# Two graph layers on one core: the small constants in ScalarE's queue, and block 1 of rows 0 multiplied by x2 in the first pass

## The chip, the cores and the metric

The kernel runs on one core of a Trainium2 chip. The time is device microseconds of one execution; the median of several executions is what two versions are compared by. All arithmetic is float32.

## What is computed

There are 4096 nodes with 128 features each, and `adj` is a dense 4096 x 4096 matrix. Two layers follow each other, each with a residual and a layer norm:

```python
# layer 1: graph convolution, layer norm, then a Mamba block over the 4096 rows
h = relu(adj @ x @ gcn_w + gcn_b)
h = (h - mean(h)) * rsqrt(var(h) + 1e-5) * ln_g + ln_b
xz = h @ w_in                              # 128 -> 512: xc and z
u  = silu(causal_conv4(xc) + conv_b)
dt = softplus((u @ w_xp)[:, :8] @ w_dt + b_dt);  B, C = the next 16 + 16 columns
hst = exp(dt * A) * hst + dt * B * u       # a scan over the rows, 256 x 16 states
y  = (hst @ C + u * D_skip) * silu(z)
x1 = layernorm(x + y @ w_out)
# layer 2: the same adj against x1 and against x2, a 3-layer MLP each, then a merge
out1 = mlp(W1, b1, (2 + eps1) * (adj @ x1));  out2 = mlp(W2, b2, (2 + eps2) * (adj @ x2))
out  = layernorm(x1 + concat(out1, out2) @ Wm.T + bm)
```

So `adj` has to be multiplied by three 4096 x 128 operands: x, x2 and x1. The first two are known from the start. Of x1, 512 rows become known each time that a chunk of the scan is done.

## The kernel before

**Tiling.** `adj` (transposed) is cut in 8 x 8 blocks of 512 x 512, 1 MB each. A block in `LOADS` is written (parts, n, m): n is the stripe of 512 result rows, m the stripe of 512 operand rows, and the parts are the operands it is multiplied by: `X` = x, `X2` = x2, `X1` = x1, `ONE` = x and x2 from one load, `DOUBLE` = x2 and x1 from one load. One part of a block is 4 matmuls of 128x128 against 128x512 (`JT` = 4). The profile writes each such float32 matmul as two (x2). A block of one part is 4 matmuls per megabyte loaded, a block of two parts is 8.

**Ring.** SyncE (SP) loads the blocks in the order of `LOADS` into four places of `ring`; load i waits until block i-4 has been used (`s_blk_used`). Blocks 0 and 1 come in four pieces each.

**The ramp.** Rows 0 of `adj @ x` (blocks 0 to 7) are computed first, since the whole chain of chunk 0 depends on them. `BOTH` = 1 says that of these only block 0 is multiplied by x2 too. VectorE (DVE) copies that partial sum of x2 out of its PSUM bank into `kept`, and it is added when the other x2 parts of rows 0, for m = 1 to 7, are done in chunk 3. Behind the ramp stand the steps gcn, in_x, x_proj and dt of chunk 0, filled up with 32 matmuls of `FILL_BLOCKS`.

**Chunks.** Chunk c is 512 rows of the scan: 16 units, one for each state, of which each takes exponentials of ScalarE (ACT, `p_dA`), two scans and a product of DVE, and two multiplications or additions of GpSimd (POOL). TensorE (PE) works on the matrix blocks at the same time: `CHUNK_BLOCKS[c]` names the blocks of each chunk, `spread_blocks` cuts their matmuls into 32 halves of units so that each half has about the same share of matmuls and steps, and `chain_steps` says in which half each of the other PE steps stands. For chunk c these are `z` of c, `out` of c-1 (c-1's y by w_out), then `gcn`, `in_x`, `x_proj` and `dt` of c+1, and the four steps of an x2 MLP, `mlp0` to `mlp3`. Each engine runs its own program in its written order. Between the PE steps of chunk c+1 the work goes through the other engines: from `gcn` to `in_x` through DVE (`stats`, lines 1102 to 1112), ACT (`norm`, 782 to 794), DVE (`turn`, 1117) and ACT (`moves`, 803, into `hr`); from `dt` to the next scans through ACT (850 to 858) and DVE (1141, 1148).

**The end of a chunk.** DVE ends unit 15 with the addition behind `mlp3` (line 1171, into `resid`) and begins unit 0 of the next chunk with two scans (line 1035). ACT follows each scan with the next exponential (line 737), and then, where a sum of x1 parts in `p_two` was closed in the unit before (`SUMS`), copies it out (line 974, `acc`). The second matmul of step `z` (line 605) writes `p_two` and so waits for this copy (`sum_taken(last_two(n, 0))`).

**Constants.** Six small loads, `w_dt` twice (9 x 256), `scale1`, `scale2` (128 x 1), `bm`, `gb` (128 x 128), stand in SP's queue between the loads of block 7 and block 8. ACT's queue holds the loads of x (and x2 for block 0) and the first part of `pack`; behind these ACT loads a table and waits for `pack`.

Of the kernel before, what the change touches and what calls it, by code (L numbers as in the profile page):

```python
# [13 lines left out]
JT = T // P  # L14
# [3 lines left out]
R = 8  # L18
# [8 lines left out]
KEEP = 5  # L27
EPS = 1e-5
PIECES = 2
BOTH = 1  # L30
END_ACT = range(2)
STAGES = 4
MOVES_0 = 2
# [6 lines left out]
ROW_DT = (0, 64)  # L40
# [19 lines left out]
def row(what, n, columns):  # L60
    return [(what, n, m) for m in columns]
# [3 lines left out]
ONE, X, X2, X1, DOUBLE = ("x", "x2"), ("x",), ("x2",), ("x1",), ("x2", "x1")  # L65


def mixed(*lists):
# [12 lines left out]
    row(ONE, 3, ALL[2:]) + row(ONE, 4, ALL[:4]),  # L81
    row(ONE, 4, ALL[4:]) + row(X, 5, ALL) + row(X1, 2, (0, 1)) + row(X, 6, (0,)) + row(X1, 3, (0, 1)),
    row(X, 6, (1,)) + row(X1, 4, (0, 1)) + mixed(row(X, 6, ALL[2:]), row(X2, 0, (3, 4, 5)))
    + row(X2, 0, (6, 7, 1, 2)) + row(X1, 0, (0, 1, 2)) + row(X, 7, (0,)),
    row(X, 7, (1,)) + row(DOUBLE, 1, (0, 1)) + mixed(row(X, 7, ALL[2:]), row(X2, 1, ALL[4:])) + row(DOUBLE, 1, (2, 3))
    + row(X1, 5, (0,)),
    row(X2, 5, (0,)) + row(DOUBLE, 5, ALL[1:4]) + row(X1, 5, (4,)) + row(X2, 5, (4, 5)) + row(X1, 2, (2, 3, 4)) + row(X2, 5, (6, 7))
# [184 lines left out]
def two_layer_graph_kernel(nc, blocks, x_d, x2_d, pack_d, w_dt_d, eps1_d, eps2_d, bm_d, gb_d, rows_d, out_d):  # L272
    ctx = ExitStack()
    with ctx:
# [38 lines left out]
        w_dt = sb("w_dt", [P, G * P])  # L313
# [153 lines left out]
        @block.sync  # L467
        def _(sp_):
            def load(i):
                _, n, m = LOADS[i]  # L470
                wait(sp_, s_blk_used, i - RING + 1)
                sp_.dma_start(ring[:, i % RING, :, :], blocks[n, m]).then_inc(s_blk[i % RING], 16)

            def load_x2(k):
                sp_.dma_start(x2_s[:, JT * k:JT * (k + 1), :], x2_d[k]).then_inc(s_x2s[k], 16)


            for i in range(PIECES):
                for jt in range(JT):
                    sp_.dma_start(ring[:, i, jt, :], blocks[0, i, :, jt]).then_inc(s_tile[JT * i + jt], 16)  # L480
            for k in range(PIECES, NBLK):
                load(k)
            for row in ROW_DT:
                sp_.dma_start(w_dt[row:row + R + 1, :], w_dt_d).then_inc(s_wdt, 16)
            sp_.dma_start(scale1[:, :], eps1_d).then_inc(s_consts_in, 16)
            sp_.dma_start(scale2[:, :], eps2_d).then_inc(s_consts_in, 16)
            sp_.dma_start(bm[:, :], bm_d).then_inc(s_consts_in, 16)
            sp_.dma_start(gb[:, :], gb_d).then_inc(s_consts_in, 16)
            for k in range(NBLK):
                load(NBLK + k)  # L490
                if k - 2 >= BOTH:
                    load_x2(k - 2)
            sp_.dma_start(pack[:, PACK_LATE:PACK_W], pack_d[:, PACK_LATE:PACK_W]).then_inc(s_late, 16)
            for k in range(NBLK - 2, NBLK):
                load_x2(k)
            for i in range(2 * NBLK, len(LOADS)):
                load(i)
            for k in range(NC - 2):
                sp_.wait_ge(s_fin, k + 1)
                sp_.dma_start(out_d[k], stage(k)).then_inc(s_out[k % STAGES], 16)  # L500
            k = NC - 1
            for h in range(2):
                tiles = slice(h * JT // 2, (h + 1) * JT // 2)
                sp_.wait_ge(s_fin_dve, h + 1)
                sp_.dma_start(out_d[k][:, tiles, :], stage(k)[:, tiles, :]).then_inc(s_out[k % STAGES], 16)
            for q in range(STAGES):
                sp_.wait_ge(s_out[q], 16 * (NC // STAGES + (q == k % STAGES)))

        @block.tensor
        def _(pe):  # L510
# [49 lines left out]
            def block_part(i, lo, hi, chunk=NC - 1, unit=S):  # L560
                steps = block_steps(LOADS[i])
                if lo == 0 and i >= PIECES:
                    pe.wait_ge(*filled(i))
                for q in range(lo, hi):
                    part, jt = steps[q]
                    last = second(i, jt, chunk, unit) if part == "x1" else first(i, part, jt)
                    if q == len(steps) - 1:
                        last.then_inc(s_blk_used, 1)
                    elif part in ("x", "x2") and jt == JT - 1 and i == LAST_OF[part, LOADS[i][1]]:
                        last.then_inc(s_px if part == "x" else s_px2, 1)  # L570
# [92 lines left out]
            for k in range(1, NBLK):  # L663
                pe.wait_ge(s_xs[k], 16)
                if k < PIECES:
                    for jt in range(JT):
                        pe.wait_ge(s_tile[JT * k + jt], 16)
                        block_part(k, jt, jt + 1)
                else:
                    block_part(k, 0, JT)  # L670
            pe.wait_ge(s_pack, 16)
# [58 lines left out]
        def _(act):  # L730
# [193 lines left out]
            for k in range(1, NBLK):  # L924

                if k == 2:
                    act.wait_ge(s_tile[1], 32)
                elif k in (3, 4):
                    act.wait_ge(s_tile[3 * k - 7], 16)
                elif k > 4:  # L930
                    act.wait_ge(*filled(k - 3))
                act.dma_start(x_s[:, JT * k:JT * (k + 1), :], x_d[k]).then_inc(s_xs[k], 16)
            act.dma_start(pack[:, 0:PACK_LATE], pack_d[:, 0:PACK_LATE]).then_inc(s_pack, 16)
            act.preload_act_table_set(LOG_EXP)
            act.wait_ge(s_pack, 16)
            act.activation(A[:, :, :], w("A_log").rearrange("p (g s) -> p g s", g=G), ACT.Exp).then_inc(s_A, 1)
# [449 lines left out]
```

## Time and profile before

| what | value |
|---|---|
| median of 3 runs | 802.83 us (802.69 to 803.57) |
| the profiled execution: time / span | 801.87 / 800.1 us |
| granted clock of TensorE | 0.999 of full |
| PE, DVE, ACT, POOL busy | 791.8, 626.9, 437.9, 620.3 us |
| PE share of the chain that ended last | 93% |
| DMA moved | 231.6 MB, mean 289 GB/s |

The span lies inside the time: 1.77 us of the profiled execution are around it. Rows begin with the start in us and the duration; a bracket at the end says how long the engine had been idle before the instruction and what ended that. PEld is TensorE's weight load, which runs beside the matmuls. An idle time that ends in "issue" is one in which nothing that the profile shows was waited for.

### The profile page before, as it was taken

The numbers are of one execution on the slowest core, as the hardware profiler recorded it, in microseconds if no ns is written. First come the engines' busy times: TensorE is split into PE (matmuls) and PEld (weight loads), VectorE is DVE, ScalarE is ACT, GpSimd is POOL, SyncE is SP. The second block draws the span as 40 slices with busy tenths as digits, with TensorE's granted clock in tenths as the row PEclk, the third lists the DMA queues.
The fourth block names the chain that finished last, engine by engine and source line by source line (L and its number), as shares of the span: only waits on it lengthen the run. The fifth ranks groups of instructions, "written<-read, shape, count | busy, mean of one in ns | idle before, by whom it ended". The sixth has DMA issues, their size and how long they took to land.

```text
span 800.1 us, 7650 instructions
## 1 busy us (share of the span) xinstructions
PE 791.8 (99%) x2100; PEld 364.4 (46%) x2100; DVE 626.9 (78%) x882; ACT 437.9 (55%) x827; POOL 620.3 (78%) x300
## 2 busy tenths in 40 slices
PE   9999999999999999999999999999999999999996
PEld 4444444444454444544454445444544454444454
DVE  0045989999998988989999998988989888982135
ACT  0165576477647764676467645863475646331235
POOL 0004999999998989899989997979789899980036
PEclk9999999999999999999999999999999999999999
DMA  8999767775766999999979977899778896887602
GB/s 334 373 342 366 234 251 252 255 255 214 266 217 193 359 378 359 339 368 375 369 255 366 374 265 246 318 349 381 262 262 290 299 349 215 303 314 273 252 26 80
DMA packets 64254, 231.61 MB, mean 289 GB/s; under 512 B 7490, under 2 KB 8532, under 8 KB 45396
## 3 DMA queue, kind: packets, MB, share of 16 engines
q1 hardware_dynamic: 25236, 160.72, 53.2%
q10 hardware_dynamic: 38976, 70.41, 26.9%
q8 instruction: 17, 0.28, 0.1%
q14 instruction: 25, 0.20, 0.1%
HBM read 228.48 MB, written 2.62 MB: 289 GB/s over the span
## 4 chain that ended last, share of the span: by engine, by line
PE 93%; DMA 2%; ACT 2%; DVE 2%; ACTq 0%; issue 0%; DVEq 0%
PE p_x L527 51%; PE p_x L557 16%; PE p_two L557 11%; PE p_m L628 2%; PE p_m L644 2%; PE p_dA L727 2%; DMA spread_C<-bc_rows 2%; PE p_two L618 1%; PE p_m L611 1%; PE p_m L593 1%; PE p_m L648 1%; PE p_m L640 1%; PE p_two L598 1%; DMA x_s<-x_tiles 1%; PE p_m L586 1%; PE p_h L727 1%
## 5 line engine op out<-in xcount | busy, mean ns | idle before, releaser
L527 PE MATMUL p_x<-ring,x_s 128*128 128x512 f32 x1024 | 453.8, 594 | 0.2 <-DMA x_s<-x_tiles 0.2
L1281 POOL TENSOR_TENSOR bh<-spread,dtu 128x1024 f32<-128x1024 f32 x127 | 300.4, 2366 | 37.9 <-DVE bh L1224 36.1
L1290 POOL TENSOR_TENSOR y<-y,prod 128x1024 f32<-128x1024 f32 x120 | 283.2, 2360 | 47.9 <-DVE prod L1048 39.4
L527 PEld LDWEIGHTS p_x<-ring,x_s 128*128 128x128 f32 x1024 | 192.1, 190 | 243.6 <-issue 240.1
L1035 DVE TENSOR_TENSOR_SCAN p_h<-p_dA,state,bh 128x512 f32<-128x512 f32 x224 | 276.1, 1278 | 21.5 <-ACT p_dA L737 8.6
L737 ACT ACTIVATE p_dA<-dt,A 128x512 f32<-128x512 f32 x256 | 172.0, 686 | 133.2 <-DVE p_h L1035 132.5
L1048 DVE TENSOR_TENSOR prod<-p_h,spread_C 128x1024 f32<-128x1024 f32 x120 | 145.7, 1214 | 5.6 <-DMA spread_C<-bc_rows 4.6
L557 PE MATMUL p_x<-ring,x 128*128 128x512 f32 x304 | 136.9, 592 | 0.0
L557 PE MATMUL p_two<-ring,x 128*128 128x512 f32 x208 | 94.2, 593 | 0.0
L557 PEld LDWEIGHTS p_x<-ring,x 128*128 128x128 f32 x304 | 57.4, 190 | 71.6 <-issue 71.6
L432 POOL TENSOR_SCALAR dtu<-prod,mv,rstd 128x128 f32<-128x128 f32 x26 | 20.4, 802 | 59.2 <-ACT rstd L1001 59.2
L557 PEld LDWEIGHTS p_two<-ring,x 128*128 128x128 f32 x208 | 38.9, 190 | 47.5 <-issue 47.5
L1083 DVE TENSOR_TENSOR acc<-p_x,acc 128x512 f32<-128x512 f32 x17 | 11.7, 687 | 41.2 <-PE p_x L557 41.2
L1035 DVE TENSOR_TENSOR_SCAN p_h<-p_dA,bh 128x512 f32<-128x512 f32 x32 | 37.5, 1218 | 2.6 <-ACT p_dA L737 1.5
L803 ACT ACTIVATE hr<-turned 32x128 f32<-32x128 f32 x120 | 36.9, 307 | 3.2 <-DVE turned L1117 0.8
L887 ACT ACTIVATE mb<-p_m,pack 128x512 f32<-128x512 f32 x16 | 11.0, 687 | 26.2 <-PE p_m L644 25.8
L1319 POOL COPY wx<-pack 128x16 f32<-128x16 f32 x1 | 0.2, 198 | 31.0 <-DMA pack<-pack_w 31.0
L1045 DVE COPY state<-p_h 128x2 f32<-128x2 f32 x112 | 16.8, 150 | 6.6 <-DVE p_h L1035 0.5
L1073 DVE SCALAR_TENSOR_TENSOR p_m<-xcv,pack,p_m 128x512 f32<-128x512 f32 x24 | 18.0, 749 | 4.1 <-ACT p_m L820 3.6
L1207 DVE TENSOR_SCALAR pack<-pack 128x512 f32<-128x512 f32 x1 | 0.5, 486 | 24.2 <-PE p_h L674 24.2
L1073 DVE SCALAR_TENSOR_TENSOR p_two<-xcv,pack,p_two 128x512 f32<-128x512 f32 x24 | 18.1, 753 | 0.6
L1141 DVE SCALAR_TENSOR_TENSOR p_two<-p_two,dt 128x512 f32<-128x512 f32 x8 | 5.6, 700 | 15.7 <-ACT dt L854 15.7
(141 smaller groups left out, 611.1 us busy)
## 6 DMA issues: line engine op xcount, KB each, us to landing
ring<-adj_blocks SPq DMA_DIRECT2D x147, 1024.0 KB, 7.2
spread_C<-bc_rows ACTq DMA_DIRECT2D x128, 256.0 KB, 6.4
spread<-bc_rows ACTq DMA_DIRECT2D x127, 256.0 KB, 5.2
ring<-adj_blocks SPq DMA_DIRECT2D x8, 256.0 KB, 6.7
x_s<-x_tiles ACTq DMA_DIRECT2D x7, 256.0 KB, 8.9
x_s<-x_tiles SPq DMA_DIRECT2D x7, 256.0 KB, 7.6
out_tiles<-dtu SPq DMA_DIRECT2D x6, 256.0 KB, 2.0
pack<-pack_w SPq DMA_DIRECT2D x1, 640.0 KB, 8.0
```

The lines of the kernel that those rows point to most:

```text
L432: last = eng.tensor_scalar(stage(k)[:, q, :], last_r(k)[:, q, :], mv[:, k % 4, q, 0:1], rstd[:, k % 4, q:q + 1], ALU.subtract, ALU.mult)
L527: return pe.matmul(bank[:, :], tiles[:, JT * m + jt, :], ring[:, i % RING, jt, :], start=opens, stop=closes)
L557: return pe.matmul(sum_bank(no)[:, :], x1[:, m % KEEP, jt, :], ring[:, i % RING, jt, :], start=opens, stop=closes)
L727: pe.matmul(bank, W1[:, l, :], moving[:, columns], start=True, stop=True).then_inc(s_l, 1)
L737: act.activation(p_dA[g][:, :], dt_[:, c % 2, g, :], ACT.Exp, scale=A[:, g, unit:unit + 1]).then_inc(s_dA, 1)
L803: last = act.activation(hr4[Q * r:Q * (r + 1), :, Q * q:Q * (q + 1)], turned[Q * q:Q * (q + 1), :, Q * r:Q * (r + 1)], ACT.Copy)
L1035: dve.tensor_tensor_scan(p_h[:, g, :], p_dA[g][:, :], bh[:, i % 3, g, :], first, ALU.mult, ALU.add).then_inc(s_scan, 1)
L1045: dve.tensor_copy(state[:, unit, :], p_h[:, :, T - 1]).then_inc(s_state, 1)
L1048: dve.tensor_tensor(prod[:, i % 2, :, :], p_h[:, :, :], both(spread_C[:, i % SLOTS_C, :]), ALU.mult).then_inc(s_cmul, 1)
L1073: dve.scalar_tensor_tensor(out=bank[:, :], in0=xcv[:, g, k:k + T], scalar=conv_w[:, g, k:k + 1], in1=bank[:, :], op0=ALU.mult, op1=ALU.add ...
L1281: pool.tensor_tensor(bh[:, i % 3, :, :], both(spread[:, q, :]), dtu[:, c % 2, :, :], ALU.mult).then_inc(s_bmul, 1)
L1290: pool.tensor_tensor(y[:, c % 2, :, :], y[:, c % 2, :, :], prod[:, i % 2, :, :], ALU.add).then_inc(s_acc, 1)
```

## The change

Three things are changed. `BOTH` becomes 2: block 1 is now (x, x2) too. PE takes its four pieces by turns, first by x, then by x2, and DVE copies the sum out after block 1. The x2 rows for it (256 KB) are loaded in ACT's queue right behind the x rows of block 1; in SP's queue the load of these same x2 rows, after block 11, is gone. In chunk 3 the single-part block (x2, 0, 1) is dropped, and block (x, 7, 0) moves ahead of the three x1 blocks. The number of matmuls is the same; there is one block load of 1 MB less (148 instead of 149). Third, the six small constants move from SP's queue to ACT's, behind `pack`, `gb` first.

```diff
-BOTH = 1
+BOTH = 2
...
-    + row(X2, 0, (6, 7, 1, 2)) + row(X1, 0, (0, 1, 2)) + row(X, 7, (0,)),
+    + row(X2, 0, (6, 7, 2)) + row(X, 7, (0,)) + row(X1, 0, (0, 1, 2)),
...
                 load(k)
-            for row in ROW_DT:
-                sp_.dma_start(w_dt[row:row + R + 1, :], w_dt_d).then_inc(s_wdt, 16)
-            sp_.dma_start(scale1[:, :], eps1_d).then_inc(s_consts_in, 16)
-            sp_.dma_start(scale2[:, :], eps2_d).then_inc(s_consts_in, 16)
-            sp_.dma_start(bm[:, :], bm_d).then_inc(s_consts_in, 16)
-            sp_.dma_start(gb[:, :], gb_d).then_inc(s_consts_in, 16)
...
                         block_part(k, jt, jt + 1)
+                        if k < BOTH:
+                            if jt == 0:
+                                pe.wait_ge(s_x2s[k], 16)
+                            block_part(k, JT + jt, JT + jt + 1)
...
                 act.dma_start(x_s[:, JT * k:JT * (k + 1), :], x_d[k]).then_inc(s_xs[k], 16)
+                if k < BOTH:
+                    act.dma_start(x2_s[:, JT * k:JT * (k + 1), :], x2_d[k]).then_inc(s_x2s[k], 16)
             act.dma_start(pack[:, 0:PACK_LATE], pack_d[:, 0:PACK_LATE]).then_inc(s_pack, 16)
+
+            act.dma_start(gb[:, :], gb_d).then_inc(s_consts_in, 16)
+            for row in ROW_DT:
+                act.dma_start(w_dt[row:row + R + 1, :], w_dt_d).then_inc(s_wdt, 16)
+            act.dma_start(scale1[:, :], eps1_d).then_inc(s_consts_in, 16)
+            act.dma_start(scale2[:, :], eps2_d).then_inc(s_consts_in, 16)
+            act.dma_start(bm[:, :], bm_d).then_inc(s_consts_in, 16)
```

How PE's program moves is shown by its instruction order (lines up to 660 of the kernel before are 6 higher than in the changed one). An `x17` is 17 matmuls; x2_s and its bank p_x2 are written as x_s and p_x. First the ramp, on PE, from the start, before:

```order
L655 MATMUL p_m<-sq 128x256 x4
L527 MATMUL p_x<-ring,x_s 128x512 x36
L674 MATMUL p_h<-pack 128x1 x4
L586 MATMUL p_m<-pack,ax 128x128 x4
L527 MATMUL p_x<-ring,x_s 128x512 x11
```

and now:

```order
L649 MATMUL p_m<-sq 128x256 x4
L521 MATMUL p_x<-ring,x_s 128x512 x40
L672 MATMUL p_h<-pack 128x1 x4
L580 MATMUL p_m<-pack,ax 128x128 x4
L521 MATMUL p_x<-ring,x_s 128x512 x11
```

Four matmuls more stand ahead of the first chunk's chain; what stands behind them is the same. Second, PE in chunk 3, from `gcn` (L586) through `in_x` (L593, L598), `x_proj` (L611) and `dt` (L618) to `mlp0` (L640), before:

```order
L586 MATMUL p_m<-pack,ax 128x128 x4
L527 MATMUL p_x<-ring,x_s 128x512 x17
L593 MATMUL p_m<-hr,pack 128x512
L598 MATMUL p_two<-hr,pack 128x512
L527 MATMUL p_x<-ring,x_s 128x512 x15
L611 MATMUL p_m<-u,wx 64x512 x2
L527 MATMUL p_x<-ring,x_s 128x512 x8
L618 MATMUL p_two<-dbc,w_dt 128x512
L618 MATMUL p_m<-dbc,w_dt 128x512
L527 MATMUL p_x<-ring,x_s 128x512 x11
L640 MATMUL p_m<-ax,pack 128x512
```

and now (the same steps under L580, L587, L592, L605, L612, L634):

```order
L580 MATMUL p_m<-pack,ax 128x128 x4
L521 MATMUL p_x<-ring,x_s 128x512 x15
L587 MATMUL p_m<-hr,pack 128x512
L592 MATMUL p_two<-hr,pack 128x512
L521 MATMUL p_x<-ring,x_s 128x512 x15
L605 MATMUL p_m<-u,wx 64x512 x2
L521 MATMUL p_x<-ring,x_s 128x512 x7
L612 MATMUL p_two<-dbc,w_dt 128x512
L612 MATMUL p_m<-dbc,w_dt 128x512
L521 MATMUL p_x<-ring,x_s 128x512 x11
L634 MATMUL p_m<-ax,pack 128x512
```

Two matmuls are gone between `gcn` and `in_x`, one between `x_proj` and `dt`. Third, PE at the end of chunk 3, from `mlp2` (L644) through `mlp3` (L648) to `z` of chunk 4 (L603, L605), before:

```order
L644 MATMUL p_m<-mb,pack 128x512
L557 MATMUL p_two<-ring,x 128x512 x3
L527 MATMUL p_x<-ring,x_s 128x512 x2
L648 MATMUL p_m<-pack,mb 128x128 x4
L527 MATMUL p_x<-ring,x_s 128x512 x5
L603 MATMUL p_m<-hr,pack 128x512
L605 MATMUL p_two<-hr,pack 128x512
```

and now:

```order
L638 MATMUL p_m<-mb,pack 128x512
L551 MATMUL p_two<-ring,x 128x512 x4
L642 MATMUL p_m<-pack,mb 128x128 x4
L551 MATMUL p_two<-ring,x 128x512 x2
L521 MATMUL p_x<-ring,x_s 128x512 x3
L597 MATMUL p_m<-hr,pack 128x512
L599 MATMUL p_two<-hr,pack 128x512
```

One matmul is gone ahead of `mlp3`; between `mlp3` and `z` there are five as before, but the x1 sum in `p_two` is closed two matmuls behind `mlp3`. From `z` to `gcn` of this chunk there are 10 matmuls as before (three now, four before, ahead of `out`).

## Rows read from the trace of the kernel before

**Rows 1.** The page, part 1: busy time, share, instructions.

```profile
PE 791.8 (99%) x2100; PEld 364.4 (46%) x2100; DVE 626.9 (78%) x882; ACT 437.9 (55%) x827; POOL 620.3 (78%) x300
```

**Rows 2.** Timeline of PEld in the ramp.

```profile
15.62 0.19 PEld L527 LDWEIGHTS p_x<-ring,x_s 128*128 128x128 f32 x1 [0.24 <-issue]
16.20 0.47 PEld L527 LDWEIGHTS p_x<-ring,x_s 128*128 128x128 f32 x2 [0.39 <-issue]
```

**Rows 3.** Waits of PEld, whole span: waited for, us in total, times, longest.

```profile
PEld p_x L527 <- issue: 240.1, 969, 0.8
...
PEld p_x L527 <- DMA x_s<-x_tiles: 3.0, 4, 1.0
PEld p_m L593 <- ACT hr L803: 1.6, 2, 1.0
```

**Rows 4.** Timeline of PE in chunk 3.

```profile
328.94 14.76 PE L527 MATMUL p_x<-ring,x_s 128*128 128x512 f32 x34
343.54 1.02 PE L593 MATMUL p_m<-hr,pack 128*128 128x512 f32 x2
...
397.53 1.02 PE L605 MATMUL p_two<-hr,pack 128*128 128x512 f32 x2
398.39 3.60 PE L527 MATMUL p_x<-ring,x_s 128*128 128x512 f32 x8
```

**Rows 5.** Timeline of PE, the ramp and the first chain.

```profile
8.65 28.59 PE L527 MATMUL p_x<-ring,x_s 128*128 128x512 f32 x66 [0.18 <-DMA x_s<-x_tiles]
...
48.74 1.13 PE L593 MATMUL p_m<-hr,pack 128*128 128x512 f32 x2
49.70 1.02 PE L598 MATMUL p_two<-hr,pack 128*128 128x512 f32 x2
```

**Rows 6.** Busy time by engine in the ramp; last: granted clock, DMA share, GB/s.

```profile
10.00:15.00 5.00, 5.00 (x13) 2.28 (x12) 0.69 (x1) 0.00 (x0) 0.00 (x0) 1.00 1.01 404
```

**Rows 7.** Timeline of the queues of SP and ACT, and ACT, 22 to 33 us.

```profile
23.91 0.72 SPq L484 DMA_DIRECT2D w_dt<-w_dt_rows  x2
...
26.02 0.43 SPq L488 DMA_DIRECT2D gb<-gcn_b_in  x1
...
26.98 10.63 SPq L472 DMA_DIRECT2D ring<-adj_blocks  x4
...
32.92 0.23 ACT L936 ACTIVATE A<-pack 128x32 f32<-128x32 f32 x1 [8.34 <-DMA pack<-pack_w]
```

**Rows 8.** Busy time by engine in chunk 3, first `z` to next `z`.

```profile
315.70:396.67 80.97, 80.96 (x215) 36.88 (x214) 74.42 (x99) 51.82 (x99) 75.38 (x33) 1.00 0.97 362
```

**Rows 9.** Timeline of DVE in chunk 3, where it waited for PE.

```profile
323.10 0.69 DVE L1152 TENSOR_TENSOR dbc<-p_m,x_s 128x512 f32<-128x512 f32 x1 [0.51 <-PE p_m L628]
...
329.14 0.70 DVE L1102 SCALAR_TENSOR_TENSOR p_m<-gb,p_m 128x512 f32<-128x512 f32 x1 [0.30 <-PE p_m L586]
...
370.75 0.70 DVE L1141 SCALAR_TENSOR_TENSOR p_two<-p_two,dt 128x512 f32<-128x512 f32 x1 [0.99 <-ACT dt L854]
...
392.58 0.69 DVE L1171 TENSOR_TENSOR resid<-p_m,bm 128x512 f32<-128x512 f32 x1 [0.75 <-PE p_m L648]
393.19 2.46 DVE L1035 TENSOR_TENSOR_SCAN p_h<-p_dA,state,bh 128x512 f32<-128x512 f32 x2
```

**Rows 10.** Timeline of ACT in chunk 3.

```profile
341.55 0.31 ACT L803 ACTIVATE hr<-turned 32x128 f32<-32x128 f32 x1
...
366.21 0.45 ACTq L756 DMA_DIRECT2D spread_C<-bc_rows  x1
367.45 0.60 ACT L850 ACTIVATE dt<-p_two 128x512 f32<-128x512 f32 x1 [0.92 <-PE p_m L618]
...
396.66 0.60 ACT L974 ACTIVATE acc<-p_two 128x512 f32<-128x512 f32 x1 [0.29 <-issue]
```

**Rows 11.** Timeline of POOL, last addition of chunk 3.

```profile
387.52 2.37 POOL L1290 TENSOR_TENSOR y<-y,prod 128x1024 f32<-128x1024 f32 x1
```

## Prediction, made before the run

> **What bounds the kernel now.** I read the busy line first, then the waits of the weight load, then stretches of the timeline. PE is busy 99% of the span [rows 1]. A busy PE need not be a full one, so I look at the weight loads: one every 0.43 us, 0.19 busy and 0.24 idle that ends in "issue" [rows 2], 969 times on this line [rows 3]. 34 passes (17 matmuls) take 14.6 us from their start to the start of the next row [rows 4], again 0.43 each. So a matmul costs two passes, 0.858 us, and PE gives one after the other without a gap in nearly all of the span. The true waits are few: 3.0 us on the operands of the first block, 1.6 us in two waits for `hr` [rows 3]. As long as the other engines deliver in time, the time is PE's work plus these, and moving four matmuls from one place to another changes nothing. The question is whether the others deliver in time in the stretch that becomes shorter.
>
> The Trainium skill, "Perfetto Trace Analysis", section "Identifying Performance Opportunities", says that headroom on the tensor engine is to be judged by the busy share of the weight loads, and on Vector and GpSimd by occupancy. By the first PE would be half empty (46%), and the four matmuls might go in free; this trace disagrees, since a pass comes each 0.43 us for 28.59 us on end [rows 5].
>
> **The ramp: +3.43 us, -0.15 us.** Four matmuls more stand ahead of `gcn` of chunk 0: 4 x 0.858 = 3.43 us. The whole first chain stands behind them, and it has the same 32 filler matmuls, so nothing hides them there; they are owed back by chunk 3. What the ramp may win: PE waits for the operands of block 0 until 8.65 [rows 5]. These are ahead of the new x2 load in ACT's queue, so this stays. The weight load at 16.20 comes 0.15 later than the cadence (0.39 instead of 0.24 idle, [rows 2]), where block 2 begins; block 1 now takes 6.86 us instead of 3.43, and block 2 has landed by then: -0.15. The 256 KB more at 3 us, at the 404 GB/s that the full DMA engines move there [rows 6], may push block 1's last pieces and block 2 back by 0.65 us. Block 1's last piece is now needed 2.6 us later than before and block 2 3.4 us later, so this is hidden; without that cover it would cost up to 0.65. The wait of PE for `hr` at 48.74 (the next row starts 0.96 behind it instead of 0.86, [rows 5]) is set by the chain from `gcn` on and moves with it.
>
> **The six constants: 0.** SP issues them from 23.91 until 26.45 and issues block 8 at 26.98 [rows 7]. The four ring loads from there on take their places from PE, one each 3.43 us; block 8 waits for block 4's end, and that is what sets 26.98. So SP loses nothing to them now and wins nothing. On ACT they take the same 2.5 us of issue behind `pack`; ACT has nothing to do but a table load until `pack` lands, an idle time of 8.34 us ending at 32.92 [rows 7]. The first step that needs them stands behind `gcn`, past the ramp's end at 8.65 + 28.59 = 37.24 [rows 5], and 3.4 us later than that now. Without that cover: up to 2.5 us. The Trainium skill, "DMA: Bandwidth & Descriptors", section "Issuing engines are not separate DMA queues", says that DMAs of all engines share the same DMA engines and that another issuer saves only issue time. By that rule the edit is worth nothing either, because the issue time saved on SP was already free.
>
> **The 1 MB and the x2 load less on SP: 0.** In chunk 3 PE waits for no ring load: its rows follow each other at the cadence, and it is busy 80.96 of 80.97 us [rows 8].
>
> **Chunk 3: -3.43 us wanted, -1.60 us got.** This is the term that decides. The chunk lasts 80.97 us and PE fills it; DVE is busy 74.42, POOL 75.38 [rows 8]. To give back the whole 3.43 us DVE must run it in 77.54. Its busy time would allow that, but what it can give up are only its waits for PE: 0.51 at `out`, 0.30 at `gcn`, 0.99 at `dt`, 0.75 at `mlp3`, 2.55 in all [rows 9]. The rest of its idle time is semaphore latency between dependent instructions. Now in order:
> - From `z` to `gcn` there are 10 matmuls before and after, so `gcn` comes at the same moment, and DVE, at 329.14, begins no earlier: the 0.51 and 0.30 are not recovered. All four matmuls go behind this point.
> - `in_x`: 15 matmuls instead of 17, so PE is there at 343.54 - 1.72 = 341.82. `hr` is ready at 341.55 + 0.31 = 341.86 [rows 10]. PE waits 0.1 and loses 0.1 more on restart (as at 48.74). It is 1.5 ahead. DVE has no idle time of PE's making from here to `dt`, so it stays where it was.
> - `dt`: one matmul less, PE is 2.4 ahead. ACT waited 0.92 for it at 367.45, but is held until 366.66 by its own queue [rows 10]: about 0.75 gained. DVE waited 0.99, so it takes all 0.75.
> - `mlp3`: one more matmul less, PE is 3.2 ahead. DVE, 0.75 early, would have been free at 392.58 - 0.75 = 391.83 before and is free at 391.08 now. The result has long been there, so it loses no further time: the addition starts 1.50 earlier than before. POOL's last addition (387.52 + 2.37 = 389.89, [rows 11]) comes before that.
> - `z` of chunk 4: two scans from 393.19 - 1.50, then ACT's exponentials, then the copy of `p_two` at 396.66 - 1.50 = 395.16, done at 395.76 [rows 9, 10]. PE's second matmul of `z` would be due at 397.53 - 3.2 = 394.3 [rows 4]; it waits until about 395.8. Before, this copy ended at 397.26, just in time. The next matmul comes at 395.83 + 0.96 = 396.79 instead of 398.39: PE has won 1.60 us.
> From there DVE and PE are both 1.5 to 1.6 us earlier than before, in the same relation as before, and the rest of the kernel is unchanged. The 1.83 us that PE waits is not given back, since no later stretch has PE waiting.
>
> **Sum.** 3.43 - 0.15 - 1.60 = +1.68 us, on the profiled execution's own 801.87: 803.55. The median of before stands 0.96 above the profiled one, so in these terms 802.83 + 1.68 = 804.5. Bounds of the chunk-3 term: at worst nothing comes back (-0), at best all of it (-3.43). I take the replay since its rows are of this very chunk.
>
> **Rivals.**
> 1. *DVE has room, all is given back* (the other side of my forecast). If the short gaps between DVE's instructions shrink when PE is early, 6.55 us (80.97 - 74.42, [rows 8]) are there, more than the 3.43. Then the copy of `p_two` is in time, PE wins 3.43 in chunk 3, and 3.43 - 0.15 - 3.43 = -0.15: 802.7. With the wait for `hr` near 100 us gone as well (1.0 the longest, 0.7 above the usual gap, [rows 3]; SP has 256 KB less to load ahead of it) 801.9. The decisive point is whether ACT's copy starts at its old distance from `mlp3` or from DVE's scans. Against it: DVE's gaps in these rows are the same wherever PE was ahead. The rule on occupancy of the page "Perfetto Trace Analysis" would make this come out.
> 2. *The lag is not contained.* If PE, early at `in_x`, `mlp0` and `z`, waits at each, and ACT, which takes the MLP copies in its order, falls late, nothing comes back: 3.43 - 0.15: 806.1. For it: at 341.86 and 395.8 the slack is already used up. Against: at `dt` ACT and DVE had waited for PE, 0.92 and 0.99 [rows 9, 10], so an earlier PE pulls them along there.
> 3. *The start suffers.* The new load in ACT's queue and the constants behind `pack` delay an operand of the ramp by up to 0.65: on top of my sum 805.2. For it: the transfers there are saturated. Against: every operand is now needed later.
>
> **How the numbers follow.** Forecast as worked out 0.58 (own range 803.8 to 805.2); rival 1 0.24 (801.9 to 803.3, the ground between it and mine included); rival 2 0.08; rival 3 0.10. 0.2% is 1.6 us, about what a measurement of this kernel tells from no change; my +1.68 lies just on that line. So of my own case half is slower and half the same; rivals 2 and 3 are slower; rival 1 is nearly all the same. Slower 0.29 + 0.08 + 0.09 = 0.46, faster 0.06, same 0.48. The time is that of the likeliest case, 804.5; the range 802.5 to 806.0 leaves out about 2 in 10.
>
> **What would show it.** In the profile after: `gcn` of chunk 0 3.2 to 3.4 us later; in chunk 3 a wait of PE at `z` of chunk 4 of some 1.5 us that ends with ACT's copy into `acc`, a small one at `in_x`, and DVE without waits for PE at `mlp3`; `z` to `z` of chunk 3 about 79.4 us instead of 80.97. It is wrong if that stretch is near 77.5 us (rival 1) or near 81 (rival 2), or if PE waits in the ramp between 8.65 and its end.

## The result, and the profile after

| | before | after |
|---|---|---|
| median | 802.29 us (801.43 to 803.57, 15 runs) | 803.65 us (803.37 to 806.65, 15 runs) |
| profiled execution, time / span | 801.87 / 800.1 us | 803.89 / 802.1 us |

The ratio after / before is 1.0018 [1.0012, 1.0025]: 1.4 us slower by the medians, 2.0 by the profiled executions. The forecast was +1.68.

The page's part 1 for the changed kernel has the busy times of [rows 1] within 0.6 us, and 2.0 us more span:

```profile
span 802.1 us, 7649 instructions
PE 791.9 (99%) x2100; PEld 363.9 (45%) x2100; DVE 626.6 (78%) x882; ACT 438.0 (55%) x827; POOL 619.8 (77%) x300
```

So PE does the same work, and the difference must be waits. The waits of the weight load over the whole span (waited for, us in total, times, longest; the rows that answer to [rows 3]) name one that has grown by more than 2 us, the second:

```profile
PEld p_x L521 <- DMA x_s<-x_tiles: 3.4, 4, 1.3
PEld p_two L599 <- ACT acc L981: 3.0, 2, 2.0
PEld p_m L587 <- ACT hr L801: 2.5, 3, 1.0
PEld p_two L612 <- ACT dbc L844: 2.3, 3, 0.8
```

Before, the wait for `acc` came to 0.8 us in all. Where PE falls behind is best read by placing each step of its program beside the same step of before. The table gives, for the weight load of some steps, how many us later it starts in the changed kernel's profile than in that of before. It is worked out from the start times of the same weight loads in both traces, and the same is done for the experiments below. Each of the steps `z` and `in_x` has two matmuls, and the head says which is meant. The offset of a load that has just waited can be up to 0.3 us larger than what PE has lost, since the loads run ahead of the matmuls; what is lost for good is read where nothing waits.

| kernel | `gcn` of chunk 0 | `in_x` 1, second | `z` 3, first | `z` 3, second | `in_x` 4, first | `z` 4, second | `in_x` 5, second | last `out` |
|---|---|---|---|---|---|---|---|---|
| changed | 3.54 | 3.51 | 3.52 | 4.26 | 2.62 | 2.13 | 2.01 | 2.01 |

**The ramp.** PE, changed kernel, the end of the ramp and `in_x` of chunk 0; it answers to [rows 5]. In the kernel before, the row of `p_h` stands at 37.08.

```profile
40.62 0.95 PE L672 MATMUL p_h<-pack 128*128 128x1 f32 x8
...
52.28 1.12 PE L587 MATMUL p_m<-hr,pack 128*128 128x512 f32 x2
53.24 1.02 PE L592 MATMUL p_two<-hr,pack 128*128 128x512 f32 x2
```

and its weight load where the matmuls begin to run without a gap:

```profile
8.75 0.30 PEld L521 LDWEIGHTS p_x<-ring,x_s 128*128 128x128 f32 x2 [0.73 <-DMA x_s<-x_tiles]
```

From 8.75 to 40.62 are 31.87 us, where 8.65 to 37.08 were 28.43: 3.44 more, the four matmuls. The other 0.10 is the later operand of block 0. The step `in_x` behind it is 3.54 later too (52.28 against 48.74, [rows 5]), with the same 0.96 from the first of its rows to the next.

**`z` of chunk 3.** Here PE loses 0.50 us that the prediction did not have. ACT, changed kernel (ACTq is the issue of a DMA in ACT's queue; the exponential issued before it still runs beside it, and what stands behind it in ACT's program comes after it):

```profile
318.24 0.69 ACT L735 ACTIVATE p_dA<-dt,A 128x512 f32<-128x512 f32 x1 [0.48 <-DVE p_h L1042]
318.25 0.33 ACTq L746 DMA_DIRECT2D spread<-bc_rows  x1
318.61 1.18 ACTq L754 DMA_DIRECT2D spread_C<-bc_rows  x1
319.84 0.60 ACT L981 ACTIVATE acc<-p_two 128x512 f32<-128x512 f32 x1 [0.91 <-DVE prod L1055]
```

and the same issue in the kernel before:

```profile
315.09 0.44 ACTq L756 DMA_DIRECT2D spread_C<-bc_rows  x1
315.58 0.60 ACT L974 ACTIVATE acc<-p_two 128x512 f32<-128x512 f32 x1 [0.17 <-issue]
```

The issue took 1.18 us instead of 0.44, and the copy behind it started 0.74 later. The bracket names DVE's `prod`, but the copy starts just where the issue ends (318.61 + 1.18 = 319.79), so that is what held it. PE's next matmul behind `z` starts at 321.45 where it started at 317.43: PE is now 4.02 late instead of 3.52. In another profiled execution of the same kernel (below) `z` was not held.

**Chunk 3.** [rows 8] runs from the first matmul of `z` to the first of the next. A wait at the second one falls behind that window, so here are windows from the second matmul of `z` to the second of the next, before and then changed (us; busy of PE, PEld, DVE, ACT, POOL; clock, DMA share, GB/s):

```profile
316.57:397.53 80.96, 80.95 (x215) 36.88 (x214) 74.41 (x99) 51.92 (x98) 75.53 (x34) 1.00 0.97 361
```

```profile
320.49:399.44 78.95, 77.78 (x206) 35.20 (x207) 73.56 (x99) 51.95 (x99) 74.23 (x33) 1.00 0.98 359
```

78.95 us instead of 80.96, where the forecast had 79.4: 2.01 given back, not 1.60. From first `z` to first `z` it is 78.03 (319.23 to 397.26), since the wait is not in it. PE is no longer busy throughout. PE at the end of this chunk, beside [rows 4], and the weight load of the waiting step:

```profile
397.26 1.02 PE L597 MATMUL p_m<-hr,pack 128*128 128x512 f32 x2
399.44 1.12 PE L599 MATMUL p_two<-hr,pack 128*128 128x512 f32 x2 [1.16 <-ACT acc L981]
```

```profile
399.44 0.30 PEld L599 LDWEIGHTS p_two<-hr,pack 128*128 128x128 f32 x2 [1.99 <-ACT acc L981]
```

The weight load runs ahead of the matmuls: it waits 1.99 us, the matmul starts 2.18 behind the one before instead of 0.86, so 1.32 is lost, and 0.1 more on the restart (the next row starts 0.96 behind it), 1.42 together. The other 2.01 of the 3.43 us is what the chunk gave back; at `in_x` of this chunk a weight load waited 0.56, but the matmul came on its cadence (345.84, 2.30 late, which is 4.02 less two matmuls), so nothing was lost there. ACT, which releases it, beside [rows 10]:

```profile
396.75 0.69 ACT L735 ACTIVATE p_dA<-dt,A 128x512 f32<-128x512 f32 x1 [3.89 <-DVE p_h L1042]
397.93 0.69 ACT L735 ACTIVATE p_dA<-dt,A 128x512 f32<-128x512 f32 x1 [0.48 <-DVE p_h L1042]
397.93 0.33 ACTq L746 DMA_DIRECT2D spread<-bc_rows  x1
398.30 0.44 ACTq L754 DMA_DIRECT2D spread_C<-bc_rows  x1
398.79 0.60 ACT L981 ACTIVATE acc<-p_two 128x512 f32<-128x512 f32 x1 [0.17 <-issue]
```

The copy waits for nothing of its own. Ahead of it in ACT's program stand two exponentials, each of which waits for a scan of DVE, and two DMA issues. It starts 3.35 us behind the start of DVE's scans (395.44, next fence), where it started 3.47 behind them before: it has kept its distance from the scans. And DVE, beside [rows 9]:

```profile
373.84 0.70 DVE L1148 SCALAR_TENSOR_TENSOR p_two<-p_two,dt 128x512 f32<-128x512 f32 x1 [0.27 <-ACT dt L852]
...
394.84 0.68 DVE L1178 TENSOR_TENSOR resid<-p_m,bm 128x512 f32<-128x512 f32 x1
395.44 2.46 DVE L1042 TENSOR_TENSOR_SCAN p_h<-p_dA,state,bh 128x512 f32<-128x512 f32 x2
```

The waits for PE at `dt` (0.99) and `mlp3` (0.75) have shrunk to 0.27 and to nothing, as forecast. The one at `gcn` has grown from 0.30 to 1.16 (0.92 in the repeated profile, where `z` 3 was not held). From the same addition a chunk earlier (315.14) to this one (394.84) DVE took 79.70 us, 80.96 before. Behind `z` 4 PE's offset stays at 2.01 to the end.

### The profile page after: what moved, and what is told of

Read it like the earlier page. It is cut to its first block, busy times and chain, and to the rows that moved or that the text cites. A ratio compares the mean times of both kernels' runs of the same rounds, so it can differ in the third digit from the quotient of the medians.

```text
span 802.1 us, 7649 instructions
## 1 busy us (share of the span) xinstructions
PE 791.9 (99%) x2100; PEld 363.9 (45%) x2100; DVE 626.6 (78%) x882; ACT 438.0 (55%) x827; POOL 619.8 (77%) x300
## 3 DMA queue, kind: packets, MB, share of 16 engines
HBM read 227.43 MB, written 2.62 MB: 287 GB/s over the span
## 4 chain that ended last, share of the span: by engine, by line
PE 83%; DVE 9%; ACT 4%; DMA 2%; issue 1%; ACTq 0%; DVEq 0%
PE p_x L521 43%; PE p_x L551 16%; PE p_two L551 10%; DVE p_h L1042 4%; DVE prod L1055 2%; PE p_m L622 2%; PE p_dA L725 2%; DMA spread_C<-bc_rows 2%; PE p_m L638 1%; PE p_two L612 1%; ACT hr L801 1%; PE p_m L605 1%; PE p_two L599 1%; PE p_m L587 1%; PE p_m L642 1%
## 5 line engine op out<-in xcount | busy, mean ns | idle before, releaser
L622 PEld LDWEIGHTS p_m<-pack,y 128*128 128x128 f32 x128 | 15.5, 192 | 3.8 <-issue 3.8
L864 ACT ACTIVATE rstd<-mv,eps_t 128x4 f32<-128x4 f32 x8 | 2.4, 297 | 27.2 <-DVE mv L1101 27.2
```

Source lines behind the costliest of these rows:

```text
L622: last = pe.matmul(p_m4[:, t, :], y[:, n % 2, g, P * t:P * (t + 1)], w_out[:, g, :], start=g == 0, stop=g == G - 1)
```

## The experiments

A short name stands for each kernel; each ratio is to the kernel before measured together with it. "Copy first" and the others are edits of the changed kernel where nothing else is said.

| kernel | median us (range) | ratio to before |
|---|---|---|
| block only | 803.94 (803.31 to 805.27) | 1.0010 [1.0000, 1.0021] |
| constants only | 802.87 (802.14 to 804.17) | 1.0000 [0.9991, 1.0009] |
| copy first | 802.49 (801.75 to 802.97) | 0.9994 [0.9985, 1.0003] |
| before, copy first | 802.23 (801.84 to 803.9) | 0.9993 [0.9984, 1.0001] |
| three blocks | 807.05 (806.07 to 808.33) | 1.0062 [1.0048, 1.0076] |
| three blocks, copy first | 804.85 (804.47 to 805.49) | 1.0032 [1.0021, 1.0044] |
| block moved back | 803.19 (802.66 to 803.66) | 1.0010 [1.0002, 1.0019] |
| old order | 803.59 (803.06 to 804.35) | 1.0015 [1.0006, 1.0024] |
| changed, again | 804.14 (803.35 to 806.91) | 1.0023 [1.0014, 1.0032] |
| copy first, again | 802.43 (801.74 to 803.65) | 0.9994 [0.9981, 1.0007] |
| before with constants and copy first | 802.35 (801.54 to 806.46) | 0.9996 [0.9982, 1.0010] |

The kernel before had a median of 802.83 beside the first four rows, 802.19 beside the next four and 802.57 beside the last three. The offsets, made as above:

| kernel | `gcn` 0 | `in_x` 1, second | `z` 3, first | `z` 3, second | `in_x` 4, first | `z` 4, second | `in_x` 5, second | last `out` |
|---|---|---|---|---|---|---|---|---|
| block only | 3.71 | 5.32 | 5.32 | 5.33 | 3.92 | 3.48 | 3.36 | 3.36 |
| constants only | 0.49 | 0.42 | 0.45 | 0.84 | 0.60 | 0.49 | 0.60 | 0.60 |
| copy first | 3.50 | 3.09 | 3.00 | 2.92 | 1.60 | -0.63 | 0.18 | -0.14 |
| before, copy first | 0.32 | 0.81 | 0.73 | 0.65 | 0.73 | 0.53 | 0.73 | 0.74 |
| three blocks | 6.95 | 6.90 | 6.88 | 6.89 | 4.63 | 4.29 | 4.17 | 4.17 |
| three blocks, copy first | 7.45 | 7.49 | 7.40 | 7.32 | 5.15 | 2.44 | 3.87 | 3.54 |
| block moved back | 4.01 | 4.05 | 3.98 | 4.58 | 4.34 | 4.23 | 4.59 | 1.75 |
| old order | 3.68 | 3.35 | 3.39 | 3.60 | 2.07 | 1.67 | 1.55 | 1.55 |
| changed, again | 4.04 | 3.81 | 4.03 | 4.03 | 2.70 | 2.24 | 2.12 | 2.12 |
| copy first, again | 4.09 | 3.89 | 3.89 | 3.81 | 2.72 | 0.48 | 1.37 | 1.05 |
| before with constants and copy first | 0.16 | -0.25 | -0.34 | -0.42 | -0.34 | -0.55 | -0.34 | -0.34 |

### Block only

`BOTH` = 2 and chunk 3 as in the changed kernel; the six constants stay in SP's queue.

```diff
+            for row in ROW_DT:
+                sp_.dma_start(w_dt[row:row + R + 1, :], w_dt_d).then_inc(s_wdt, 16)
+            ...
+            sp_.dma_start(gb[:, :], gb_d).then_inc(s_consts_in, 16)
...
-            act.dma_start(gb[:, :], gb_d).then_inc(s_consts_in, 16)
-            ...
```

> Only the second x2 block in the first pass; the six constants stay in SP's queue. Theory A (the loss is four matmuls that go to the ramp, +3.5 us, and of which chunk 3 gives back only part, because PE waits at z of chunk 4 for ACT's copy of p_two): the whole effect is here, as in the changed kernel, +1.3 to +2.1 us over the kernel before, with PE's idle time before the weight load of the second z matmul of chunk 4 near 2 us. Rival B (the loss comes from ACT's queue, which the constants lengthen): here +0.0 to +0.5 us.

Its median is 1.11 us above the kernel before, a little under the 1.3 expected, and the interval reaches from nothing to 1.7 us, so the time alone does not rule out rival B. The wait does place the loss here: 2.04 us at `z` 4, as in the full change. The profile is 1.6 us worse in chunk 0: DVE waited there for a load of `spread_C` (256 KB) that every kernel waits for, but here 6.41 us, where such waits came to 4.6 in the profile of before and 4.9 in that of the changed kernel:

```profile
82.17 1.22 DVE L1054 TENSOR_TENSOR prod<-p_h,spread_C 128x1024 f32<-128x1024 f32 x1 [6.41 <-DMA spread_C<-bc_rows]
```

This execution (805.27) is the slowest of its kernel, so its offset of 3.36 is not the edit's price; the median is.

### Constants only

The kernel before with the six loads behind `pack` in ACT's queue, the reverse of the edit above.

```diff
-            for row in ROW_DT:
-                sp_.dma_start(w_dt[row:row + R + 1, :], w_dt_d).then_inc(s_wdt, 16)
-            ...
+            act.dma_start(gb[:, :], gb_d).then_inc(s_consts_in, 16)
+            ...
```

> Only the six constants move to ACT's queue; block 1 is multiplied by x alone, as before. Theory A: nothing on PE's path, within 0.3 us of the kernel before; pack lands some us earlier or later, and block 8 lands earlier than its 12.2 us after issue, with no change in the start of in_x of chunk 0. Rival B: +1 us or more.

No difference: 1.0000, and an offset near 0.5 in all stages, which is the kind of difference that two executions of one kernel have ("changed, again" against "changed": 0.5 at `gcn` 0). So rival B of the run above, the longer queue of ACT, is out. What the trace shows besides is the landing of block 8, the first ring load behind the place of the constants. The issues of `ring` in a window from the issue of block 8 (KB, us to landing), before and then with the constants moved:

```profile
ring<-adj_blocks SPq DMA_DIRECT2D x1, 1024.0 KB, 12.2
```

```profile
ring<-adj_blocks SPq DMA_DIRECT2D x1, 1024.0 KB, 9.3
```

It lands 2.9 us sooner, and PE wins nothing by it, for it does not wait for this block in either kernel. With `BOTH` = 2 the same block, issued at 30.68 with the constants ahead of it (block only) and at 30.51 without (changed), landed 9.9 and 7.8 us after its issue.

### Copy first, in both kernels

In unit 0 of a chunk ACT copies the closed sum `p_two` before the exponentials, instead of behind them. Done to the changed kernel and to the kernel before.

```diff
+                    def take_sums():
+                        for no in sums_here(c, unit):
+                            ...   # wait for s_blk_used, copy into acc2
+                    if unit == 0:
+                        take_sums()
                     if unit < S - 1:
                         decay(c, unit + 1)
...
-                    for no in sums_here(c, unit):
-                        ...
+                    if unit:
+                        take_sums()
```

> The changed kernel, but in unit 0 of a chunk ACT copies the closed x1 sum out of p_two ahead of the exponentials of the next unit, not behind them and their two DMA issues. Theory A1 (the 2 us that PE waits at z of chunk 4 are the order of ACT's program: the copy is ready to be made but stands behind exponentials that wait for DVE's scans; DVE's own lag of about 1.5 us fits into the slack of in_x, x_proj and dt in chunk 4, where DVE waits for PE by 2 to 3 us): PE does not wait at z, chunk 3 gives back 3.0 to 3.4 us, and the time falls by 1.5 to 2.3 us below the changed kernel, to about that of the kernel before (-0.3 to +0.4). Rival A2 (DVE is the bound of chunk 3, PE would wait for it at the next place anyway, at in_x or x_proj of chunk 4): the wait moves there and the time stays within 0.5 us of the changed kernel.

> The kernel before with the same move of ACT's copy as in the run on the changed kernel. There the copy ended at 397.26 and PE's second z matmul began on its cadence at 397.53, so both A1 and A2 expect nothing: within 0.3 us of the kernel before. A gain of more than 0.5 us would mean that the copy already cost time before the change.

The edit removes the loss from the changed kernel. In the kernel before it shows no clear gain: the median is 0.60 us lower, more than either theory expected, but the interval has 1 in it, and in the profile PE runs at its cadence through `z` 3 and `z` 4 with and without the edit and ends 0.7 later with it. ACT and then PE at the end of chunk 3, changed kernel with the copy first:

```profile
393.87 0.60 ACT L971 ACTIVATE acc<-p_two 128x512 f32<-128x512 f32 x1 [2.04 <-PE p_two L551]
395.72 0.69 ACT L735 ACTIVATE p_dA<-dt,A 128x512 f32<-128x512 f32 x1 [1.25 <-DVE p_h L1048]
```

```profile
396.25 1.02 PE L597 MATMUL p_m<-hr,pack 128*128 128x512 f32 x2
397.10 1.02 PE L599 MATMUL p_two<-hr,pack 128*128 128x512 f32 x2
397.96 3.60 PE L521 MATMUL p_x<-ring,x_s 128*128 128x512 f32 x8
```

The copy stands in idle time of ACT, and now waits only for the matmuls whose sum it takes. The second matmul of `z` follows at the cadence, 0.85 behind the first. PE's chunk, from second matmul to second matmul of `z` as above, is down to 77.52 us, 3.44 less than before:

```profile
319.58:397.10 77.52, 77.51 (x207) 35.28 (x206) 72.64 (x98) 51.55 (x98) 73.33 (x33) 1.00 0.98 360
```

So the whole four matmuls are given back: the offset falls from 3.00 at `z` 3 to -0.43 behind `z` 4 (the -0.63 of the table is a load that had waited in the kernel before). DVE does not run the chunk that fast. Its additions behind `mlp3` of chunks 2 and 3:

```profile
314.62 0.69 DVE L1184 TENSOR_TENSOR resid<-p_m,bm 128x512 f32<-128x512 f32 x1 [2.14 <-PE p_m L642]
...
393.81 0.68 DVE L1184 TENSOR_TENSOR resid<-p_m,bm 128x512 f32<-128x512 f32 x1
```

They are 79.19 us apart (80.96 before, 79.70 in the changed kernel). DVE enters chunk 4 1.23 later than in the kernel before, while PE enters it 0.43 earlier than there, and DVE makes it up: its waits for PE at `out` and `gcn` of chunk 4, 0.26 and 0.30 before, are gone, and the one at `dt` falls from 1.51 to 0.94. PE loses 0.29 more at `in_x` 5, whose second matmul writes `p_two` and follows another copy of ACT; the edit leaves that copy behind the moves into `hr`:

```profile
424.15 0.60 ACT L971 ACTIVATE acc<-p_two 128x512 f32<-128x512 f32 x1
424.86 0.30 PEld L592 LDWEIGHTS p_two<-hr,pack 128*128 128x128 f32 x2 [0.85 <-issue]
```

At the end the offset is -0.14.

### Three blocks, with the old and the new place of the copy

The change once more in the same direction: `BOTH` = 3, so eight matmuls more in the ramp than the kernel before, and (x2, 0, 2) gone from chunk 3 too.

```diff
-BOTH = 2
+BOTH = 3
-    + row(X2, 0, (6, 7, 2)) + row(X, 7, (0,)) + row(X1, 0, (0, 1, 2)),
+    + row(X2, 0, (6, 7)) + row(X, 7, (0,)) + row(X1, 0, (0, 1, 2)),
...
+                elif k < BOTH:
+                    pe.wait_ge(s_x2s[k], 16)
+                    block_part(k, 0, 2 * JT)
```

> One step further: block 2 too is multiplied by x2 in the first pass, chunk 3 has one block part less again (72 matmuls; 80 in the kernel before, 76 in the changed one). Theory A (chunk 3 can give back only what PE's early arrival frees on DVE and ACT, and that is used up): nearly all of the further 3.43 us stays, 2.4 to 3.4 us above the changed kernel, 806.0 to 807.3, with the wait at z of chunk 4 grown from 2 to about 4.5 us. Rival C (each block that goes to the ramp costs the same share, about 40% of 3.43, as the first one did): 1.2 to 1.7 us above the changed kernel, about 805.

> As the run with block 2 too, with ACT's copy of p_two ahead of the exponentials in unit 0 of a chunk. Theory A1 (behind the order of ACT's program there is DVE's own limit: with one part less PE's lead of 3.4 us fits into the slack of chunk 4; with two parts less the lead of 6.9 us does not): PE does not wait at z but at in_x of chunk 3 and chunk 4, by 1.5 to 3 us together; the time is 1.5 to 3 us above that of the changed kernel with the copy first, 804.0 to 805.5. Rival A3 (the copy's place is the only limit): all is given back, 802.5.

By the medians the second block costs 3.5 us more than the first, as if none of it came back (807.05 - 802.19 = 4.86 against 1.36); by the profiles it costs 2.2 (4.17 against 2.01). The medians fit theory A, the profiles lie between it and rival C, and five runs do not settle it. The wait at `z` 4 was expected at 4.5 us and is 2.59. The rest of the lead is lost earlier, at `dt` (L612) and `mlp0` (L634), where no wait was forecast:

```profile
369.45 0.18 PEld L612 LDWEIGHTS p_two<-dbc,w_dt 9*128 9x128 f32 x1 [1.32 <-ACT dbc L847]
...
379.80 0.30 PEld L634 LDWEIGHTS p_m<-ax,pack 128*128 128x128 f32 x2 [2.13 <-issue]
...
401.60 0.30 PEld L599 LDWEIGHTS p_two<-hr,pack 128*128 128x128 f32 x2 [2.59 <-ACT acc L984]
```

With the copy first (804.85, inside the range expected) the last of the three is gone, the first two stay, and the wait forecast for chunk 4 is there, at `in_x` 5:

```profile
370.16 0.18 PEld L612 LDWEIGHTS p_two<-dbc,w_dt 9*128 9x128 f32 x1 [1.51 <-ACT dbc L847]
...
380.30 0.30 PEld L634 LDWEIGHTS p_m<-ax,pack 128*128 128x128 f32 x2 [1.92 <-issue]
...
428.55 0.30 PEld L592 LDWEIGHTS p_two<-hr,pack 128*128 128x128 f32 x2 [1.46 <-issue]
```

```profile
427.84 0.60 ACT L974 ACTIVATE acc<-p_two 128x512 f32<-128x512 f32 x1
```

PE enters chunk 3 7.40 late, leaves `z` 4 2.65 late and is 3.55 late behind `in_x` 5 and to the end, so 3.9 us of the two block parts' 6.9 come back for good. The 0.9 us at `in_x` 5 end with a copy of ACT that was not moved; what moving it too would bring was not tried. So one block part is what this program makes room for; with the second PE runs into `dt`, `mlp0` and `in_x` 5.

### Block moved back

The four matmuls taken out of chunk 3 are put back there from chunk 4, and chunk 4 takes them from chunk 5: the debt is to be given back in chunk 5, where the waits of DVE for PE were larger.

```diff
-    + row(X2, 0, (6, 7, 2)) + row(X, 7, (0,)) + row(X1, 0, (0, 1, 2)),
-    row(X, 7, (1,)) + row(DOUBLE, 1, (0, 1)) + ...
-    + row(X1, 5, (0,)),
-    row(X2, 5, (0,)) + row(DOUBLE, 5, ALL[1:4]) + ...
+    + row(X2, 0, (6, 7, 2)) + row(X, 7, (0, 1)) + row(X1, 0, (0, 1, 2)),
+    row(DOUBLE, 1, (0, 1)) + ...
+    + row(X1, 5, (0,)) + row(X2, 5, (0,)),
+    row(DOUBLE, 5, ALL[1:4]) + ...
```

> The changed kernel, but chunk 3 keeps its 80 matmuls: block (x, 7, 1) goes from chunk 4 to chunk 3 and block (x2, 5, 0) from chunk 5 to chunk 4, so that the four matmuls are missing in chunk 5, which had 88 (84 now). ACT's copy is where it was. Theory A: PE does not get ahead of DVE in chunk 3, the wait at z of chunk 4 falls from 2 us to at most 0.3, and chunk 5, where the PE share is largest, gives back 3.0 to 3.4 us: 802.2 to 803.0, as the kernel before. Rival B2 (the ramp's loss is not given back wherever the matmuls are taken from): as the changed kernel, 803.6 to 804.

Chunk 3 keeps its length, and the wait at `z` 4 is 0.33:

```profile
401.54 0.19 PEld L599 LDWEIGHTS p_two<-hr,pack 128*128 128x128 f32 x1 [0.33 <-ACT acc L981]
403.74 0.30 PEld L551 LDWEIGHTS p_two<-ring,x 128*128 128x128 f32 x2 [0.81 <-issue]
...
459.25 0.30 PEld L551 LDWEIGHTS p_two<-ring,x 128*128 128x128 f32 x2 [1.15 <-issue]
```

Chunk 5 does give the block back (5.19 late at `mlp0` of chunk 4, 1.75 at the end: 3.44). But the order of chunk 4 that this edit makes has small waits of its own, the second and third row, at which the offset grows from 4.35 to 5.19, and the result, 803.19, is just above the range expected. Between the changed kernel and this one the intervals (1.0012 to 1.0025 and 1.0002 to 1.0019) overlap, so it is no clear gain.

### Old order

Chunk 3 with the x1 blocks ahead of (x, 7, 0) again; if the new place of that block made the wait, it should go.

```diff
-    + row(X2, 0, (6, 7, 2)) + row(X, 7, (0,)) + row(X1, 0, (0, 1, 2)),
+    + row(X2, 0, (6, 7, 2)) + row(X1, 0, (0, 1, 2)) + row(X, 7, (0,)),
```

> The changed kernel with the order of blocks at the end of chunk 3 as before: the three x1 blocks ahead of (x, 7, 0), so that the x1 sum in p_two is closed four matmuls earlier. Theory A: the copy waits for its place in ACT's program, not for PE, so nothing changes: within 0.3 us of the changed kernel, wait at z of chunk 4 near 2 us. Rival D (the late close of the sum behind mlp3 is what delays the copy): the wait shrinks by 1.7 us or more and the time falls by as much.

The wait is 2.08 us and the time that of the changed kernel. The order of these blocks is not the cause.

### The pair again, and the last combination

The changed kernel and its copy-first version beside each other, with the same chip and runs of before, and as a third the kernel before with the constants in ACT's queue and the copy first.

> The changed kernel itself, once more, as the control beside the next two on the same chip. Theory A: +1.3 to +2.0 us over the kernel before, a wait near 2 us at z of chunk 4 that ends with ACT's copy of p_two.

> The changed kernel with ACT's copy of p_two first in unit 0, once more, now beside the changed kernel. Theory A1: 1.2 to 2.0 us below the changed kernel of the same job, within 0.5 us of the kernel before. Rival A2 (DVE's lag is lost anyway): within 0.5 us of the changed kernel.

> The kernel before (block 1 of rows 0 by x alone) with the constants in ACT's queue and ACT's copy first: the two parts that cost PE nothing, without the four matmuls in the ramp. If the copy's place now and then costs time in the kernel before too (its copy ended 0.27 us before PE needed it), this is 0.2 to 0.7 us below the kernel before; else within 0.3 us. It should be no slower than the changed kernel with the copy first.

The pair is 1.71 us apart (804.14 and 802.43), so the gain of the earlier copy is not one chip's chance. In this profile of the changed kernel `z` 3 was not held by a long issue (offset 4.03 at both of its matmuls), and it still waits at `z` 4:

```profile
399.55 0.30 PEld L599 LDWEIGHTS p_two<-hr,pack 128*128 128x128 f32 x2 [2.02 <-ACT acc L981]
```

In the repeated copy-first profile there is no such wait; chunk 3 gives back 3.2 us (3.90 to 0.69) and `in_x` 5 costs 0.36.

The last combination is 0.22 us below the kernel before, which fits both cases that were written down for it. None of the copy-first kernels with one or two blocks in the ramp can be told from the kernel before: 0.9993 to 0.9996, each interval with 1 in it. No version here beats it by more than its measurement is uncertain.

## Why the prediction was right

**The sum was right**: +1.68 against +1.36 (medians) and +2.02 (profiles). In part this is luck: of the profile's +2.01 the ramp is 3.54 (forecast 3.28), a hold at `z` 3 that was not foreseen is 0.50, and chunk 3 gave back 2.01 from there (forecast 1.60), so that errors of +0.26, +0.50 and -0.41 meet. The time itself, 804.5, is 0.85 above the measured 803.65, of which 0.54 is the median of before: 802.83 in the 3 runs that the forecast had, 802.29 in 15.

**The ramp.** The four matmuls cost 3.44 for a forecast 3.43, and a later operand of block 0 cost 0.10. The small term was wrong: the 0.15 us of block 2's late weight load was not won, because it had cost nothing. The weight load runs a pass ahead of the matmuls, and 0.15 of delay is inside that lead. The changed kernel's weight loads come every 0.43 from 9.29 on, and `p_h` is still the full 3.44 later.

**The constants, the 1 MB less.** Both 0, as forecast; the constants by an experiment of their own, the 1 MB only in that PE has no new wait for a ring load.

**Chunk 3.** The replay gave -1.60; the profile's first `z` is 3.52 late when it enters and the kernel 2.01 when it leaves, so -1.51 in all, the long issue at `z` 3 included, and -2.01 from behind it. In the repeated profile it is 4.03 to 2.12, -1.91. So the term was 0.3 to 0.4 too small: `in_x` was to cost 0.2 and cost at most 0.1, `z` 4 was to cost 1.6 and cost 1.42. The step where it stops is the one named, the copy of `p_two`, which ends the wait at `z` 4 and starts at its old distance from DVE's scans. DVE was to win 1.50; it won 1.26, in the repeated profile 1.66. The sign "`z` to `z` about 79.4" holds only between second matmuls (78.95); taken as in [rows 8], at the first ones, the chunk is 78.03 and in the repeated profile 77.59, next to the 77.5 that was to speak for rival 1, and so could not tell the two apart.

**What it read too strongly.** It said that to give back the whole 3.43 us DVE must run the chunk in 77.54, and gave the way that "all is given back" the condition that DVE's gaps shrink. The copy-first runs show that neither is needed. DVE takes 79.19 us there, so it was right that DVE gives no more than its waits for PE (1.77 us, with 2.55 of such waits and 6.55 idle in all), and still PE runs its chunk in 77.52. PE may leave the chunk ahead of DVE, and DVE catches up in chunk 4, where it had waits for PE as well. DVE's scans held PE only because the copy stood behind exponentials that wait for them. For two block parts this slack was not enough in the program as written (three blocks). The remark that DVE's other idle time is latency between dependent instructions was too simple too: 1.36 us of it, at 342.70, is one wait for an exponential of ACT (1.18 in the changed kernel, ending with POOL). The Trainium skill, "Perfetto Trace Analysis", section "Identifying Performance Opportunities", takes Vector's occupancy for a fair measure of how close that engine is to its roofline. This trace had 8% of idle DVE in chunk 3 (6.55 of 80.97 us), and in no run with one more block part did DVE turn more than 1.8 us of it into a shorter chunk.

**Rival 2** (nothing comes back) and **rival 3** (the start suffers) did not happen: the wait at `in_x` 4 cost nothing and the ramp's later operand 0.1. Not foreseen was the 0.50 at `z` 3. It is the same cause in a second place: whatever delays ACT between a chunk's start and this copy goes to PE.

**Left open.** Whether the second block part costs 2.2 or 3.5 us; how much of the 1.4 to 2.0 us is the varying wait for the load of `spread_C` in chunk 0; and why the issue at `z` 3 was long in one execution.

## What to carry to other kernels

Work moved out of a full stretch of the bound engine lets the others finish that stretch sooner only by what they waited for the bound engine there: read these waits one by one, and not the busy shares. Then look at what releases the bound engine at the stretch's end. If it hangs on the others' last step, their gain is all that comes back. If it does not have to, the bound engine can run ahead of them into the next stretch, as far as there is slack. An instruction ready long before may stand in its engine's program behind others that wait; putting it first cost nothing that could be measured here and was worth the loss of one block part.

## What the runs showed of the hardware

- DMA issue on ACT's queue mostly takes 0.33 to 0.45 us here, but the same instruction took 1.18 at 318.61 and 0.82 in the copy-first kernel at 391.50. ACT's next instruction in the program came only after it (319.84 behind 319.79).
- The place of small loads in a queue matters to the large ones behind them. With the six constants (of which four are under 10 KB) moved out of SP's queue, block 8 landed 9.3 us after its issue instead of 12.2, and with `BOTH` = 2 7.8 us (changed) instead of 9.9 (block only). That cost and brought nothing, as nothing waited.
- On the other side `pack`, ahead of the constants in ACT's queue, was first used at 28.92 in the changed kernel and at 33.95 with the constants alone (32.92 before, [rows 7]), but also at 29.22 in block only, which has no constants there, and at 32.09 in copy first, whose queue is that of the changed kernel. These runs do not show that the constants move it.
- A PE that has run dry loses 0.1 us more on its restart: the next row comes 0.96 behind instead of 0.86 (at 52.28 and at 399.44 in the changed kernel).
